# Five late strips a head on VectorE, with the chain's last step in the next head

## The chip, the cores and the metric

The kernel runs on one core of one Trainium2 chip. Its time is the device time of the whole program in microseconds. TensorE is called PE here and in the rows (PEld are its weight loads), VectorE is DVE, ScalarE is ACT, GpSimd is POOL and SyncE, which issues the DMAs, is SP.

## The reference

Two blocks on x of shape (2, 2048, 512), float32: attention with a memory term, then a feed-forward product with weights and activations rounded to float8.

```python
h = layernorm(x)
q, k, v = h @ Wq.T, h @ Wk.T, h @ Wv.T            # 4 query groups x 8 heads x 16; 8 heads x 16
probs = softmax(einsum('bsqhd,bthd->bqhst', q, k) / sqrt(16))
a_dot = einsum('bqhst,bthd->bsqhd', probs, v)
sigma_q = elu(q.reshape(b, s, 4, 128))
a_mem = sigma_q @ memory / (sigma_q @ memory_norm)
x = x + a_dot * (1 - w) + a_mem * w               # w = sigmoid(memory_weight)
x = x + float8_round(layernorm(x) / s) * s @ (weight * weight_scale).T
```

For each batch, head and query group there are 2048 x 2048 scores, and every one needs an exponential. That is most of the work.

## The kernel before

**Heads and strips.** After a preparation (projections, norms, transposes) the kernel runs 64 "heads": 8 chunks of 512 query tokens (NG) times 8 attention heads. One head n computes scores of 4 query groups x 512 tokens against 2048 keys. They are cut into 64 strips; a strip is 128 keys (on the partitions) by the 512 queries of one group, 512 float32 in one bank of PSUM. Strip s has key tile s // 4 and group s % 4. Heads 0 to 62 run in the pipeline described here, the last one in a form of its own that the change leaves alone. There is no row maximum: a guard value in the operands keeps the exponent in range, and the row sum comes out of the weighing, from a column of ones beside the values.

**Units.** Most strips go in units of two or three. PE writes the scores of a unit (pair_scores, third_scores, L1028), ScalarE takes the exponential of the whole unit in one activation (L865, 1536 or 1024 elements a partition), and two or three units later PE weighs it: it multiplies the probabilities with the values into the accumulators (weigh, L1153). The table UNITS_OF_HEAD writes the row out for even and odd heads, WEIGH_BEHIND and WEIGHED_LATER say how many units later each is weighed. Units alternate between two sets of PSUM banks. A unit of two leaves its third bank free; some of these units have an extra in it: "memory" (memory_products: the memory term of half a chunk, units 0 and 2 of even heads), "product" (ffn_product: the feed-forward product of one tile of 128 tokens, unit 2 of odd heads from head 11 on; in head 7 units 2 and 4 turn the weight instead) and "late".

**Late strips.** Four units of two, units 10 to 13 of an even head and 7 to 10 of an odd one, have "late" in their third bank: one strip of the *next* head's last key tile (LATE_TILE, four strips, LATE = 4). ScalarE never sees these. VectorE takes each from PSUM (take_late, L1593) into the buffer late_x and computes the exponential of all four at once by integer and polynomial steps, called the chain: two masks (L1598, L1601), then four two-tensor steps (L1603, L1608, L1610, L1612), each over 2048 elements. The first half is chain_begin, the second chain_end; the result goes to late_probs, a part of the tensor pool. In the next head PE weighs it, one strip behind each of units 14 to 17 (weigh_late, WEIGH_LATE_AT). The step at L1608 waits until PE has weighed the late strips of the head before (late_weighed).

**What releases what.** scores(u) waits for the activation of unit u - 2. The third strip of a unit of three waits (third_free) until the extra that was in its bank has been read. held_in_third finds that extra by going back two units at a time:

```python
def held_in_third(u):
    u -= SLOTS
    while u >= SLOTS and UNITS[u].width < WIDE and UNITS[u].extra is None:
        u -= SLOTS
    return UNITS[u].extra, UNITS[u].number
```

The extras are read by VectorE: late strips by take_late, the memory term by add_memory (L1724, L1728), the feed-forward product by ffn_out (L1716), which raises y_ready. The turned weight is read by copy_ffn_weight.

**VectorE's order.** Each engine runs its instructions in the order in which they are written. VectorE's list for head n is: add_memory(n) in even heads; take_sums(n - 1), which waits until PE has weighed the whole of the head before (pv_done) and moves both accumulators out of PSUM (L1631, raises acc_read, for which PE's first weighing of head n waits); add_memory(n + 1) in even heads; add_sums(n - 1), four small steps; in even heads moments and the rounding to float8 of one tile (round_to_float8, into xq_now) or, in the first chunk, the decoding of the weight; ffn_out or copy_ffn_weight in odd heads that have one; then late_exponentials(n + 1), the four takes and the whole chain. SP turns the rounded tile by DMA (turn_tile), and waits for y_ready too.

## Time and profile before

| | us |
|---|---|
| median of 3 runs | 1939.13 |
| lowest and highest run | 1934.77, 1944.62 |
| the profiled execution | 1942.58 |
| its span, first to last instruction | 1940.5 |

| engine | busy us | share |
|---|---|---|
| PE | 1863.9 | 96% |
| ACT | 1833.6 | 94% |
| DVE | 1409.9 | 73% |
| POOL | 107.2 | 6% |

The heads fill the stretch from 170 us to the end; the preparation is before it. The granted clock of PE is 1.0 of full speed throughout. An engine's busy share is an average, and PE's ends are modelled, so what bounds a stretch is read from who waits for whom. "Idle before" a group of instructions is time of its own engine, with the instruction that ended it.

### The profile page before, as it was taken

To read this page: it belongs to the slowest core of one execution; us is meant where nothing else is said; L and a number is where in the kernel's file an instruction comes from. 1 tells how busy PE (TensorE), PEld (TensorE's weight loads), DVE (VectorE), ACT (ScalarE), POOL (GpSimd) and SP (SyncE) were. 2 spreads that over 40 slices of the span, in tenths; PEclk is the share of its full clock that TensorE was granted. 3 is DMA by queue.
4 is the path that set the end of the run, shared out by engine and by line. 5 is a ranking of instruction groups with operands and counts; after the bars stand their busy time and mean duration, and the time that the engine had idled before them with its cause. 6 is when DMAs were issued, how large, how long until landed. Compare 5 with 4: busy or idle time off the path is not lost.

```text
span 1940.5 us, 115379 instructions
## 1 busy us (share of the span) xinstructions
PE 1863.9 (96%) x54988; PEld 1162.0 (60%) x54996; DVE 1409.9 (73%) x1833; ACT 1833.6 (94%) x1596; POOL 107.2 (6%) x150
## 2 busy tenths in 40 slices
PE   8999999999999999999999999999999999999998
PEld 7885555556565555555555555555655555555555
DVE  6675777777777777787777777777777777777755
ACT  5556999999999999999999999999999999999997
POOL 5541000000000000000000000000000000000000
PEclk9999999999999999999999999999999999999999
DMA  6654111121112211222112211212112211222111
GB/s 220 201 187 153 54 54 40 45 57 45 54 41 56 78 49 42 56 58 64 47 49 56 78 47 44 57 46 76 44 53 57 78 50 41 56 50 72 43 47 46
DMA packets 131327, 130.38 MB, mean 67 GB/s; under 512 B 30451, under 2 KB 106455, under 8 KB 130855
## 3 DMA queue, kind: packets, MB, share of 16 engines
q1 hardware_dynamic: 129847, 121.15, 21.2%
q8 instruction: 431, 7.06, 1.6%
q10 hardware_dynamic: 1008, 1.84, 0.3%
q14 instruction: 41, 0.34, 0.1%
HBM read 86.96 MB, written 32.24 MB: 61 GB/s over the span
## 4 chain that ended last, share of the span: by engine, by line
ACT 76%; PE 21%; issue 2%; DVE 1%; POOL 0%; DMA 0%; ACTq 0%; DVEq 0%; POOLq 0%
ACT pool L865 74%; PE ps L1153 8%; PE ps L945 6%; PE ps L1028 4%; ACT pool L872 1%; PE ps L1200 1%; PE ps L918 1%; DMA resid<-in_x 0%; PE ps L984 0%; POOL q_sq L727 0%; PE ps L909 0%; POOL xn L704 0%; PE ps L926 0%; DVE v_tiles L1608 0%; DVE v_tiles L1610 0%
## 5 line engine op out<-in xcount | busy, mean ns | idle before, releaser
L865 ACT ACTIVATE pool<-ps 128x1536 f32<-128x1536 f32 (+1 forms) x1388 | 1710.1, 1413 | 17.0 <-PE ps L1028 14.7
L1153 PE MATMUL ps<-pool,v_st 64*32 64x128 f32 (+2 forms) x35744 | 1398.3, 357 | 14.7 <-issue 13.7
L1153 PEld LDWEIGHTS ps<-pool,v_st 64*32 64x32 f32 x35744 | 854.5, 106 | 210.0 <-issue 54.3
L1028 PE MATMUL ps<-q_st,k_st 51*32 51x512 f16 x16128 | 903.6, 381 | 49.0 <-ACT pool L865 11.6
L1028 PEld LDWEIGHTS ps<-q_st,k_st 51*32 51x32 f16 x16128 | 246.0, 89 | 474.3 <-ACT pool L865 427.5
L1593 DVE TENSOR_SCALAR late<-ps 128x512 int32<-128x512 f32 x248 | 171.6, 692 | 212.5 <-PE ps L1028 212.5
L1608 DVE SCALAR_TENSOR_TENSOR v_tiles<-late 128x2048 f32<-128x2048 f32 x62 | 142.1, 2293 | 148.1 <-PE ps L1153 144.7
L1612 DVE SCALAR_TENSOR_TENSOR pool<-v_tiles,late 128x2048 f32<-128x2048 f32 x62 | 142.1, 2292 | 2.1
L1610 DVE SCALAR_TENSOR_TENSOR v_tiles<-v_tiles,late 128x2048 f32<-128x2048 f32 x62 | 142.1, 2292 | 2.1
L1603 DVE SCALAR_TENSOR_TENSOR late<-late 128x2048 f32<-128x2048 f32 x62 | 141.6, 2285 | 0.0
L747 POOL TENSOR_TENSOR rstd<-var_eps,minus_half 128x1 f32<-128x1 f32 x32 | 23.0, 720 | 1696.8 <-DVE var_eps L1672 1696.8
L1631 DVE STREAM_TRANSPOSE by_token<-ps 128x512 f32<-128x512 f32 x126 | 82.7, 695 | 32.4 <-PE ps L1153 32.3
L1601 DVE TENSOR_SCALAR late<-late 128x2048 int32<-128x2048 int32 x62 | 76.1, 1228 | 2.1
L1598 DVE TENSOR_SCALAR late<-late 128x2048 int32<-128x2048 int32 x62 | 76.1, 1227 | 2.1
L792 ACT ACTIVATE parts<-ps 128x512 f16<-128x512 f32 x40 | 23.9, 597 | 44.0 <-PE ps L945 44.0
L1492 DVE SCALAR_TENSOR_TENSOR y_out<-epos,ps 128x512 f32<-128x512 f32 x32 | 22.0, 688 | 46.4 <-ACT epos L801 46.3
L945 PE MATMUL ps<-x_high,wqT 128*128 128x512 f32 x128 | 51.6, 403 | 0.0
L945 PE MATMUL ps<-x_high,wq_low 128*128 128x512 f32 x128 | 49.9, 390 | 0.0
L945 PE MATMUL ps<-x_low,wqT 128*128 128x512 f32 x128 | 46.2, 391 | 0.0
L1200 PE MATMUL ps<-mem_aug,wqT 128*32 128x129 f32 x1024 | 41.4, 279 | 0.3
L1728 DVE SCALAR_TENSOR_TENSOR resid<-ps,rnorm,resid 128x128 f32<-128x128 f32 x128 | 39.0, 347 | 2.3
L1200 PEld LDWEIGHTS ps<-mem_aug,wqT 128*32 128x32 f32 x1024 | 24.2, 109 | 25.2 <-DVE resid L1728 17.4
(169 smaller groups left out, 955.1 us busy)
## 6 DMA issues: line engine op xcount, KB each, us to landing
v_st<-v_aug SPq DMA_DIRECT2D x64, 256.0 KB, 3.5
q_st<-q_aug SPq DMA_DIRECT2D x127, 128.0 KB
k_st<-k_aug SPq DMA_DIRECT2D x127, 128.0 KB
sigma_kept<-y_out SPq DMA_DIRECT2D x32, 256.0 KB, 2.0
q_aug<-parts SPq DMA_DIRECT2D x32, 256.0 KB, 2.7
wqT<-sigma_kept SPq DMA_DIRECT2D x32, 256.0 KB, 3.8
q_st<-q_aug SPq DMA_DIRECT2D x127, 64.0 KB
k_st<-k_aug SPq DMA_DIRECT2D x127, 64.0 KB
```

What stands on the lines that cost most here:

```text
L865: act.activation(probs[:, u % HELD, 0:UNITS[u].width * CH], scored(u).rearrange("p a b -> p (a b)"), ACT.Exp, bias=LIFT, scale=EXP_UNIT / ...
L945: return pe.matmul(bank(c, o), w, (x_high, x_low)[x_part][:, par, k, :], start=(k == 0 and p == 0), stop=(k == KT - 1 and p == len(PASSES) ...
L1028: return pe.matmul(ps[VW * c:VW * c + VW, bank, :], k_st[RT * r:RT * r + AUG, n % 2, keys:keys + VW], q_st[RT * r:RT * r + AUG, n % 2, q * ...
L1153: last = pe.matmul(acc[r][VW * c:VW * c + VW, :].rearrange("v (i s) -> v i s", s=VW)[:, places, :], v_st[rows, n % 2, j, :], by_place[rows ...
L1200: last = pe.matmul(am[VW * c:VW * c + VW, t * (KV + 1):(t + 1) * (KV + 1)], sigma_st[:, tokens:tokens + VW], mem_aug[:, :], start=True, st ...
L1593: dve.tensor_scalar(late_x[:, x * CH:x * CH + CH].bitcast(I32), extra_bank("late", number), -2.0 ** 23 / OCTAVE, LOWEST, ALU.mult, ALU.min ...
L1598: dve.tensor_scalar(part.bitcast(I32), fixed.bitcast(I32), MANTISSA, QUARTER, ALU.bitwise_and, ALU.bitwise_or).then_inc(late_step, 1)
L1603: dve.scalar_tensor_tensor(part, part, POWER[0], part, ALU.add, ALU.mult).then_inc(late_step, 1)
L1608: dve.scalar_tensor_tensor(grown, part, POWER[1], part, ALU.add, ALU.mult).then_inc(late_step, 1)
L1610: dve.scalar_tensor_tensor(grown, grown, POWER[2], part, ALU.add, ALU.mult).then_inc(late_step, 1)
L1612: return dve.scalar_tensor_tensor(dst, grown, POWER[3], power, ALU.add, ALU.mult)
L1631: last = dve.transpose(by_token[:, r, :, :, :].rearrange("p q t v -> p (q t v)"), acc[r])
```

## The change

Five strips of each head are now late strips: the last key tile's four and the last strip of the tile before (LATE_STRIPS). The rows of units are now constants EVEN_HEAD and ODD_HEAD, each with one late unit of two more and one unit of three fewer; there are 22 units in a head as before. Head 0, which has no late strips of its own, gets 25 units instead of 24. Late units are 9 to 13 of an even head and 7 to 11 of an odd one. Late strips are weighed behind units 12 to 16. Which units are weighed one unit later is set anew.

The chain is cut differently. late_powers is the first half, late_polynomial two steps of the second, with wait for late_weighed as before; both steps write to late_probs itself instead of late_y, which is gone. The last step is a function of its own, finish_late(n), called in the list of head n, not in that of head n - 1: first in even heads, and between take_sums and add_sums in odd ones. xq_now has moved into the place of k_sq, and pool and late have new sizes.

```diff
-LATE_TILE = ST - 1
-LATE = QG
+HEAD_STRIPS = ST * QG
+LATE_STRIPS = tuple(range(HEAD_STRIPS - QG, HEAD_STRIPS)) + (HEAD_STRIPS - QG - 1,)
+LATE = len(LATE_STRIPS)
...
-UNITS_OF_HEAD = (["2memory", "3", "2memory"] + ["3"] * 7 + ["2late"] * 4 + ["3"] * 8,
-                 ["3", "3", "2product", "3", "2spare", "3", "3"] + ["2late"] * 4 + ["3"] * 11)
+EVEN_HEAD = ["2memory", "3", "2memory"] + ["3"] * 6 + ["2late"] * LATE + ["3"] * 8
+ODD_HEAD = ["3", "3", "2product", "3", "2spare", "3", "3"] + ["2late"] * LATE + ["3"] * 10
 WEIGH_BEHIND = 2
-WEIGHED_LATER = ((0, 1, 2), (0, 1, 2, 3, 9))
-WEIGH_LATE_AT = 14
+WEIGHED_LATER = ((0, 1, 2, 10, 11, 12), (0, 1, 2, 3))
+WEIGH_LATE_AT = 12
...
+def forms_of_head(n):
+    if n == 0:
+        return ["2"] * EARLY_UNITS + EVEN_HEAD[:-1] + ["2", "2"]
+    return (EVEN_HEAD, ODD_HEAD)[n % 2]
...
-            def chain_end(step, width, dst):
-                power, part, grown = late_x[:, 0:width], late_z[:, 0:width], late_y[:, 0:width]
+            def late_polynomial(step):
                 dve.wait_ge(late_step, step + 3)
-                dve.scalar_tensor_tensor(grown, part, POWER[1], part, ALU.add, ALU.mult).then_inc(late_step, 1)
+                dve.scalar_tensor_tensor(late_probs, late_z, POWER[1], late_z, ALU.add, ALU.mult).then_inc(late_step, 1)
                 dve.wait_ge(late_step, step + 4)
-                dve.scalar_tensor_tensor(grown, grown, POWER[2], part, ALU.add, ALU.mult).then_inc(late_step, 1)
-                dve.wait_ge(late_step, step + 5)
-                return dve.scalar_tensor_tensor(dst, grown, POWER[3], power, ALU.add, ALU.mult)
+                dve.scalar_tensor_tensor(late_probs, late_probs, POWER[2], late_z, ALU.add, ALU.mult).then_inc(late_step, 1)
...
-                chain_begin((n - 1) * CHAIN_STEPS, LATE * CH)
-                if n == 1:
-                    for par in range(2):
-                        dve.wait_ge(v_stored[par], 16 * (NG // 2 + 1))
-                else:
+                late_powers((n - 1) * CHAIN_STEPS)
+                if n > 1:
                     dve.wait_ge(late_weighed, n - 1)
-                chain_end((n - 1) * CHAIN_STEPS, LATE * CH, late_probs).then_inc(late_ready, 1)
+                late_polynomial((n - 1) * CHAIN_STEPS)
+
+            def finish_late(n):
+                dve.wait_ge(late_step, n * CHAIN_STEPS)
+                dve.scalar_tensor_tensor(late_probs, late_probs, POWER[3], late_x, ALU.add, ALU.mult).then_inc(late_ready, 1)
...
                 if n % 2 == 0:
+                    if n > 0:
+                        finish_late(n)
                     add_memory(n)
                 if n > 0:
                     take_sums(n - 1)
                 if n % 2 == 0:
                     add_memory(n + 1)
+                else:
+                    finish_late(n)
                 if n > 0:
                     add_sums(n - 1)
```

VectorE where an odd head with a feed-forward product begins, before; by_token is the target of take_sums, head_out of add_sums, y_out that of ffn_out:

```order
L1612 SCALAR_TENSOR_TENSOR pool<-v_tiles,late 128x2048 [waits late_step]
L1631 STREAM_TRANSPOSE by_token<-ps 128x512 [waits pv_done]
L1631 STREAM_TRANSPOSE by_token<-ps 128x512
L1637 TENSOR_TENSOR head_out<-by_token 128x272 [waits acc_read]
L1640 RECIPROCAL rden<-head_out 128x16 [waits halves_added]
L1642 TENSOR_TENSOR head_out<-head_out,rden 128x16x16 [waits rden_ready]
L1647 TENSOR_TENSOR resid<-resid,head_out 128x4x4x16 [waits head_out_ready]
L1716 SCALAR_TENSOR_TENSOR y_out<-ps,scalars,resid 128x512 [waits y_stored,ffn_ready]
```

The same place of VectorE's order now:

```order
L1636 STREAM_TRANSPOSE by_token<-ps 128x512 [waits pv_done]
L1636 STREAM_TRANSPOSE by_token<-ps 128x512
L1631 SCALAR_TENSOR_TENSOR pool<-pool,late 128x2560 [waits late_step]
L1642 TENSOR_TENSOR head_out<-by_token 128x272 [waits acc_read]
L1645 RECIPROCAL rden<-head_out 128x16 [waits halves_added]
L1647 TENSOR_TENSOR head_out<-head_out,rden 128x16x16 [waits rden_ready]
L1652 TENSOR_TENSOR resid<-resid,head_out 128x4x4x16 [waits head_out_ready]
L1721 SCALAR_TENSOR_TENSOR y_out<-ps,scalars,resid 128x512 [waits y_stored,ffn_ready]
```

The chain's last step has moved from ahead of take_sums to behind it, and so stands between take_sums and all that follows.

PE at unit 6 of such a head, before (L1028 writes scores, a pair in 8 products and a third strip in 4; L1153 weighs):

```order
L1028 MATMUL ps<-q_st,k_st 32x512 [waits probs_ready]
L1028 MATMUL ps<-q_st,k_st 32x512 x7
L1028 MATMUL ps<-q_st,k_st 32x512 [waits y_ready]
L1028 MATMUL ps<-q_st,k_st 32x512 x3
L1153 MATMUL ps<-pool,v_st 32x384 [waits probs_ready]
L1153 MATMUL ps<-pool,v_st 32x384 x7
L1153 MATMUL ps<-pool,v_st 32x128 [waits probs_ready]
L1153 MATMUL ps<-pool,v_st 32x128 x15
```

PE at unit 6 now:

```order
L1034 MATMUL ps<-q_st,k_st 32x512 [waits probs_ready]
L1034 MATMUL ps<-q_st,k_st 32x512 x7
L1034 MATMUL ps<-q_st,k_st 32x512 [waits y_ready]
L1034 MATMUL ps<-q_st,k_st 32x512 x3
L1159 MATMUL ps<-pool,v_st 32x384 [waits probs_ready]
L1159 MATMUL ps<-pool,v_st 32x384 x7
L1159 MATMUL ps<-pool,v_st 32x128 [waits probs_ready]
L1159 MATMUL ps<-pool,v_st 32x128 x15
```

Here nothing has moved: the third strip of unit 6 waits for the reading of the feed-forward product, before and now.

VectorE where an even head begins, before, from the end of the late chain to the first part of the memory term (rnorm, resid):

```order
L1608 SCALAR_TENSOR_TENSOR v_tiles<-late 128x2048 [waits late_step,late_weighed]
L1610 SCALAR_TENSOR_TENSOR v_tiles<-v_tiles,late 128x2048 [waits late_step]
L1612 SCALAR_TENSOR_TENSOR pool<-v_tiles,late 128x2048 [waits late_step]
L1724 RECIPROCAL rnorm<-ps 128x2 [waits am_ready]
L1728 SCALAR_TENSOR_TENSOR resid<-ps,rnorm,resid 128x128 [waits rnorm_ready]
```

And now:

```order
L1614 SCALAR_TENSOR_TENSOR pool<-late 128x2560 [waits late_step,late_weighed]
L1616 SCALAR_TENSOR_TENSOR pool<-pool,late 128x2560 [waits late_step]
L1631 SCALAR_TENSOR_TENSOR pool<-pool,late 128x2560 [waits late_step]
L1729 RECIPROCAL rnorm<-ps 128x2 [waits am_ready]
L1733 SCALAR_TENSOR_TENSOR resid<-ps,rnorm,resid 128x128 [waits rnorm_ready]
```

In an even head the last step keeps its place in the row; the steps are wider and write to another tensor.

## Rows read from the trace of the kernel before

**Rows 1.** The page: busy time of each engine over the span.

```profile
PE 1863.9 (96%) x54988; PEld 1162.0 (60%) x54996; DVE 1409.9 (73%) x1833; ACT 1833.6 (94%) x1596; POOL 107.2 (6%) x150
```

**Rows 2.** Waits, 480 to 1870 us: us in total, times, longest.

```profile
PEld ps L1028 <- ACT pool L865: 340.7, 723, 0.8
...
ACT pool L865 <- PE ps L1028: 10.8, 19, 2.0
```

**Rows 3.** Timeline of ScalarE: start us, us, engine, line, what.

```profile
1008.24 1.12 ACT L865 ACTIVATE pool<-ps 128x1024 f32<-128x1024 f32 x1
...
1011.90 1.54 ACT L865 ACTIVATE pool<-ps 128x1536 f32<-128x1536 f32 x1
...
1025.23 1.23 ACT L865 ACTIVATE pool<-ps 128x1024 f32<-128x1024 f32 x1
```

**Rows 4.** Heads 31 and 30 as stretches: us, busy of each engine.

```profile
1022.57:1050.52 27.95, 26.55 (x853) 16.39 (x845) 17.85 (x18) 27.46 (x23) 0.00 (x0) 1.00 0.21 59
995.43:1022.57 27.14, 26.48 (x867) 15.80 (x866) 23.00 (x33) 27.09 (x24) 0.72 (x1) 1.00 0.15 42
```

**Rows 5.** Groups by line and shape: busy us, mean ns | idle before.

```profile
L865 ACT ACTIVATE pool<-ps 128x1536 f32<-128x1536 f32 x1008 | 1387.5, 1525 | 16.7 <-PE ps L1028 14.5
...
L865 ACT ACTIVATE pool<-ps 128x1024 f32<-128x1024 f32 x380 | 385.9, 1118 | 0.3 <-PE ps L1028 0.3
...
L1593 DVE TENSOR_SCALAR late<-ps 128x512 int32<-128x512 f32 x248 | 171.6, 692 | 212.5 <-PE ps L1028 212.5
L1608 DVE SCALAR_TENSOR_TENSOR v_tiles<-late 128x2048 f32<-128x2048 f32 x62 | 142.1, 2293 | 148.1 <-PE ps L1153 144.7
...
L1598 DVE TENSOR_SCALAR late<-late 128x2048 int32<-128x2048 int32 x62 | 76.1, 1227 | 2.1
```

**Rows 6.** Timeline of VectorE around the start of odd head 31.

```profile
1024.31 1.31 DVE L1631 STREAM_TRANSPOSE by_token<-ps 128x512 f32<-128x512 f32 x2 [0.84 <-PE ps L1153]
...
1027.22 0.74 DVE L1716 SCALAR_TENSOR_TENSOR y_out<-ps,scalars,resid 128x512 f32<-128x512 f32 x1
```

**Rows 7.** Timeline of ScalarE: units 0 and 6 of head 31.

```profile
1022.57 1.63 ACT L865 ACTIVATE pool<-ps 128x1536 f32<-128x1536 f32 x1
...
1029.86 1.54 ACT L865 ACTIVATE pool<-ps 128x1536 f32<-128x1536 f32 x1
```

**Rows 8.** Timeline at PE's unit 6 (PEld: weight loads), heads 31, 61.

```profile
1028.76 0.13 PEld L1028 LDWEIGHTS ps<-q_st,k_st 51*32 51x32 f16 x12 [0.34 <-ACT pool L865]
...
1028.99 0.38 PE L1028 MATMUL ps<-q_st,k_st 51*32 51x512 f16 x1
...
1847.72 0.74 DVE L1716 SCALAR_TENSOR_TENSOR y_out<-ps,scalars,resid 128x512 f32<-128x512 f32 x1
...
1849.27 0.13 PEld L1028 LDWEIGHTS ps<-q_st,k_st 51*32 51x32 f16 x12 [0.33 <-ACT pool L865]
```

**Rows 9.** Timeline at the memory bank of even head 32.

```profile
1051.50 0.61 DVE L1728 SCALAR_TENSOR_TENSOR resid<-ps,rnorm,resid 128x128 f32<-128x128 f32 x2
...
1052.38 0.13 PEld L1200 LDWEIGHTS ps<-mem_aug,wqT 128*32 128x32 f32 x4 [0.53 <-DVE resid L1728]
```

**Rows 10.** Timeline: scores of PE and the activation that waited.

```profile
1034.43 0.38 PE L1028 MATMUL ps<-q_st,k_st 51*32 51x512 f16 x2
...
1035.27 1.45 ACT L865 ACTIVATE pool<-ps 128x1536 f32<-128x1536 f32 x1 [0.20 <-PE ps L1028]
```

**Rows 11.** Chain in order of time: start us, us, what.

```profile
1032.05 0.67 PE ps L1153 x15
...
1033.08 0.52 PE ps L1153 x25
```

**Rows 12.** Who waited for the turned weight's tile: us, times.

```profile
  PEld ps L1210: 1.3, 1
```

**Rows 13.** Timeline of VectorE, late chain in head 31.

```profile
1044.44 2.29 DVE L1608 SCALAR_TENSOR_TENSOR v_tiles<-late 128x2048 f32<-128x2048 f32 x1 [4.62 <-PE ps L1153]
...
1049.10 2.29 DVE L1612 SCALAR_TENSOR_TENSOR pool<-v_tiles,late 128x2048 f32<-128x2048 f32 x1
```

More of the change, by code:

```diff
@@ L99, in extra_of @@
     return None, 0
+def forms_of_head(n):
+    if n == 0:
+        return ["2"] * EARLY_UNITS + EVEN_HEAD[:-1] + ["2", "2"]
+    return (EVEN_HEAD, ODD_HEAD)[n % 2]
 def units_of(n):
     units, strip, names = [], 0, []
-    for form in ["2"] * EARLY_UNITS * (n == 0) + UNITS_OF_HEAD[n % 2]:
+    for form in forms_of_head(n):
         width, name = int(form[0]), form[1:]
@@ L238, in attention_ffn @@
         k_sq = sb("k_sq", [P, CH], BF16)
+        xq_now = k_sq
         v_tiles = sb("v_tiles", [P, 2, HEADS, TPC, VW], F32)
@@ L245, in attention_ffn @@
         sigma_st = wqT[:, 0, :].bitcast(F32)
-        late_y = v_tiles[:, :, :, :, :].rearrange("p a h t w -> p (a h t w)")
         wkv_raw = sb("wkv_raw", [P, 2, DM], F32)
@@ L284, in attention_ffn @@
             v_turn = early("v_turn", [P, CH], F32)
-        pool = sb("pool", [P, 8192], F32)
+        pool = sb("pool", [P, (HELD * WIDE + LATE) * CH], F32)
         late = sb("late", [P, 2 * LATE * CH], F32)
@@ L292, in attention_ffn @@
         xqT = sb("xqT", [P, KT, P], BF16)
-        xq_now = sb("xq_now", [P, DM], BF16)
         probs = pool[:, 0:HELD * WIDE * CH].rearrange("p (a b) -> p a b", a=HELD)
@@ L1144, in late_scored @@
                     pe.wait_ge(operands_loaded[n % 2], (n // 2 + 1) * 16 * SCORE_LOADS)
-                third_scores(u, n, LATE_TILE * QG + x).then_inc(late_scores, 1)
+                third_scores(u, n, LATE_STRIPS[x]).then_inc(late_scores, 1)
             def weigh(n, j, held, first_strip, strips, first=False, last_strips=False):
@@ L1177, in weigh_late @@
                 pe.wait_ge(late_ready, n)
-                last = weigh(n, LATE_TILE, late_probs[:, x * CH:x * CH + CH], x, 1)
+                j, q = divmod(LATE_STRIPS[x], QG)
+                last = weigh(n, j, late_probs[:, x * CH:x * CH + CH], q, 1)
                 if x == LATE - 1:
@@ L1594, in take_late, with late_powers @@
                                   -2.0 ** 23 / OCTAVE, LOWEST, ALU.mult, ALU.min).then_inc(late_taken, 1)
-            def chain_begin(step, width):
-                fixed, part = late_x[:, 0:width], late_z[:, 0:width]
+            def late_powers(step):
+                fixed, part = late_x, late_z
                 dve.tensor_scalar(part.bitcast(I32), fixed.bitcast(I32), MANTISSA, QUARTER,
```

## The prediction

> **What bounds the kernel now.** I read the page first: ScalarE is busy 94% of the span, VectorE 73% [rows 1]. PE shows 96%, but its ends are modelled, so the waits decide: the weight loads of PE's scores wait 340.7 us for ScalarE in the 1390 us in the middle, ScalarE waits 10.8 us for those scores [rows 2]. So ScalarE's row of exponentials is the clock. Then its cadence: four activations of 1024 elements from 1008.24 to 1011.90, ten of 1536 to 1025.23 [rows 3]: 0.915 us for a unit of two strips, 1.33 us for one of three. A head (16 wide and 6 narrow units) should last 26.8 us; an even head lasts 27.14 us and the odd one after it 27.95 us [rows 4]. The 0.3 to 1.1 us over is time in which ScalarE waited.
>
> **The strip taken from ScalarE.** In heads 1 to 62 one wide unit becomes a narrow one: 62 x (1.33 - 0.915) = 62 x 0.415 = **-25.7 us**. Head 0 keeps its 64 strips but in 25 units: three more narrow, two fewer wide, 3 x 0.915 - 2 x 1.33 = +0.1 us. The mean durations (1525 against 1118 ns [rows 5]) give 0.407 each, the other bound: -25.2 us. The Trainium skill, page "ScalarE: Activation LUTs", section "What ACT_TABLE_LOAD costs", gives 0.833 ns for each element: an estimate of 427 ns for 512 of them, and of -26.4 us for this term.
>
> **What VectorE takes on.** A head's late work grows from four strips to five. One two-tensor step of the chain goes from 2.293 us [rows 5] to 2.87 us at 5/4 of the width. From two widths (0.74 us for the 512 of ffn_out [rows 6], 2.293 for 2048) it would be 2.81, the other bound. The Trainium skill, page "VectorE: DVE Perf Modes", section "Side-by-side: where the cycles go for N=2048 bf16", counts one element a cycle and about 158 cycles more: an estimate of 2.83 us for 2560. A head's late work (4 takes of 0.69, two masks of 1.23, four steps of 2.29 [rows 5]) is 14.4 us and becomes 18.0. In a pair of heads VectorE is busy 17.85 + 23.00 = 40.9 of 55.1 us [rows 4]; then 48.1 of 54.3. In sum it fits; the order decides.
>
> **The moved step in odd heads, the term that decides.** There VectorE's order was: the chain's last step, take_sums, add_sums, the FFN result (ffn_out), then the new late strips. take_sums waited 0.84 us for PE and started at 1024.31 [rows 6], so the chain's last step ahead of it was covered and cost nothing. Now it stands behind take_sums, ahead of add_sums and ffn_out, which wait for nothing there. take_sums can't start earlier, since PE's last weighing of the head before releases it. So ffn_out ends one step of 2.87 us later. It ended at 1027.22 + 0.74 = 1027.96 [rows 6], 5.39 us after the head's first activation at 1022.57 [rows 7]; now at 8.26.
>
> Who waits for it? In PE's order the third strip of the head's seventh unit (unit 6) waits on y_ready: it writes the bank that held the FFN product (unit 4 has two strips and leaves that bank alone). PE came there at 1028.76 [rows 8], 0.80 us after ffn_out's end. In head 61, the last such, it is 1849.27 against 1847.72 + 0.74 = 1848.46 [rows 8], 0.81. So the 26 odd heads from 11 to 61 have 0.8 us of slack, and 2.87 are taken from it. Behind the waiting instruction stand PE's weighings and its next scores, and ScalarE waits for the strip itself.
>
> When does ScalarE get unit 6? Release: add_memory's last step ended at 1051.50 + 0.61 = 1052.11, PE's load that waited for it started at 1052.38 [rows 9]: 0.26 us. Strip to activation: pair and third strip started at 1034.43 and the activation that waited for them at 1035.27 [rows 10], 0.84 us, of which the pair is 0.22 (1028.76 to 1028.99 [rows 8]); so 0.62. Unit 6 starts 8.26 + 0.26 + 0.62 = 9.14 us into the head, and started at 1029.86 - 1022.57 = 7.29 [rows 7]. That is 1.85 us, x 26 = **+48.1 us**. With the shorter step it is 46.5.
>
> After that PE has no lead. It owes the third strip (0.22), a weighing of three strips (0.67), a split one (0.52) and the next pair (0.22) with 0.4 to hand over, some 2.0 us, against 0.62 + 1.33 = 1.95 of cover. Then two narrow units each ask 0.22 + 0.67 + 0.22 = 1.11 us of PE (weighings from the chain [rows 11]) against 0.915 of ScalarE, 0.2 each. I take 0.4 a head, **+10 us**; the ends are 0 and, if four of the five narrow units fall behind, 0.8 or +21.
>
> **The weight head (7).** The same shift meets the copies of the turned weight. PE waited 1.3 us for those already [rows 12], so nothing covers it: **+2.9 us**, once.
>
> **The even heads.** Here the moved step stands where it stood, ahead of add_memory, only wider. What pays for it is that late weighing now ends at unit 16, not 17. VectorE sat idle 4.62 us for that weighing and went on at 1044.44 [rows 13], 21.9 us into the head. Ahead of it lie now nine wide and seven narrow units, before eleven and six: 1.75 us less, so 20.1. The masks and the first step are done by then: before, 4.62 us earlier, at 17.25; the fifth narrow unit adds 0.9 and the wider masks and step 1.1, so 19.3. Three steps of 2.87 from 20.1 and 0.1 between them end at 28.8. This head lasts 27.95 - 0.42 = 27.5, so they end 1.3 us into the even head, before 1049.10 + 2.29 - 1050.52 = 0.87 [rows 13]. The memory bank comes free 0.45 us later. PE already waited 0.53 us for it [rows 9] without holding ScalarE. I charge 0.2 us a head for this and for the five narrow units in a row: 31 x 0.2 = **+6 us**; ends 0 and 0.45, or +14. In odd heads the late result is ready some 6 us in and wanted at unit 12, past 14 us: nothing.
>
> The chain's middle steps write elsewhere at the same width, xq_now has another place, SyncE's turn of the tile waits for ffn_out and goes 2.9 us later, far ahead of its use two heads on: nothing, and no more than that step's delay if it were on the path.
>
> **The sum.** -25.7 + 0.1 + 48.1 + 10 + 2.9 + 6 = +41 us. The profiled execution took 1942.6 us (its span 1940.5), so 1984; the median of the runs shown is 3.5 us lower, so **1980 us**. Low end: -25.7 + 46.5 + 2.9 = +24, or 1963; if the 0.8 us by which the odd head exceeds the even one [rows 4] falls in part into the new wait, 0.2 x 26 less, 1958. High end: -25.2 + 48.1 + 21 + 3 + 14 = +61, or 2000; with the same 0.2 the other way about 2002 to 2005. I take 2002.
>
> **Rivals.** *The bank's release does not hold ScalarE* (faster). PE would have to reach the third strip so late that the FFN result's delay stays covered; it decides at 0.8 us, any shift under that is free. Then -25.7 + 6 + 0.1 = -20, or 1920 us. For it: ScalarE is the clock and the strip is really gone. Against it: the slack is the same 0.8 in heads 31 and 61, and the step is 2.87. 6%.
> *The delay is half absorbed* (same). take_sums had 0.84 us of idle; if PE delivered the sums earlier by all of that and lost no lead after, the wait is 1.0 us: 26 x 1.0 + 2.9 + 6 - 25.6 = +9, 1948 us, or 1943 with the 0.2 a head. Against it: what PE has to do before that weighing is unchanged. 5%.
> *VectorE becomes the clock* (much slower). If the chain ends 1 us later than worked out, memory banks and sums hold PE by that in 31 heads: +31, or 2011 us. It decides where take and masks end after 20.1 us instead of at 19.3. For it: 48.1 of 54.3 us busy. Against it: in this forecast product heads grow by 1.8 us, which gives VectorE room. 9%.
> That the change does not do what it says is ruled out by the order of instructions: steps of 2560 and five takes in each head.
>
> **How the numbers follow.** The forecast's case has 80% and the range 1958 to 2002; the rivals' centres lie outside it. 0.5%, about what a measurement of this kernel can tell from no change, is 9.7 us: faster 6%, same 5%, slower 89%.
>
> **What would show it.** ffn_out starts 2.9 us later after its head's first activation; PE's load at unit 6 names VectorE's y_out as what it waited for, some 2 us in each of 26 heads; ScalarE has a gap of 1.8 to 1.9 us ahead of unit 6 and small ones after it. Odd heads without a product and even heads last 26.6 to 27.0 us, the odd product heads 29 to 29.5. Were product heads under 27.5 us, the bank's step would be wrong; were the even heads over 27.5, the late chain's.

## The result and the profile after

| | before | after |
|---|---|---|
| median, lowest to highest of 4 runs, us | 1940.85 (1934.77 to 1944.62) | 2004.97 (2004.01 to 2008.66) |
| profiled execution | 1942.58 | 2005.04 |
| its span | 1940.5 | 2003.0 |

The ratio is 1.0337, with a 95% interval from 1.0306 to 1.0368: the kernel became slower by 64 us. I had predicted 1980 us and a range up to 2002. The direction was right, 25 us were missing, and the time lies 3 us above the range. (Before has one run more here than where the prediction was made, so its median is 1940.85 and not 1939.13.)

The page of after, busy time of each engine (answers to [rows 1]):

```profile
PE 1860.3 (93%) x56532; PEld 1240.7 (62%) x56532; DVE 1609.1 (80%) x1895; ACT 1826.8 (91%) x1597; POOL 106.9 (5%) x150
```

ScalarE is busy for 7 us less, and the span is 62 us longer: the time is in its gaps. Waits of after, 480 to 1870 us, the same view as [rows 2] (us in total, times, longest):

```profile
PEld ps L1034 <- ACT pool L871: 238.8, 505, 0.8
...
PEld ps L1159 <- issue: 76.8, 129, 2.6
ACT pool L871 <- PE ps L1034: 64.3, 85, 2.1
...
PEld ps L1034 <- DVE y_out L1721: 42.8, 25, 1.7
PE ps L1159 <- issue: 30.5, 47, 2.3
PEld ps L1034 <- issue: 25.6, 30, 2.6
```

PE's wait for ScalarE, the sign that ScalarE is the clock, fell from 340.7 to 238.8 us; ScalarE's wait for PE rose from 10.8 to 64.3 [rows 2]. Two things are new: the 42.8 us for y_out, which I had named, and the rows with "issue", waits without a releaser. In before they read:

```profile
PEld ps L1153 <- issue: 46.4, 94, 2.6
...
PE ps L1153 <- issue: 13.1, 19, 2.2
...
PEld ps L1028 <- issue: 6.1, 11, 1.4
```

Together 65.6 us before and 132.9 after. (Rows of PE and of PEld can tell of the same stretch, so these sums count some time twice; the count further down does not.) Nothing in my prediction speaks of them.

**The count by heads.** From the starts of all activations in the trace I took the time from each to the next, less 1.3425 us for a unit of three and 0.917 for one of two. (An undisturbed unit takes 1.331 and 0.904, so it counts as -0.01.) What is left is the stall ahead of the next unit. The means of even heads here and below are over heads 12 to 60 and those of product heads over 13 to 59, where nothing else is given; the differences are sums over all heads of a kind. In us:

| mean of a head | before | after | heads | difference of the sums |
|---|---|---|---|---|
| even heads | 0.13 | 1.50 (1.13 in heads 2 to 10) | 31 | +41 |
| odd heads with a product | 0.66 | 2.33 | 26 | +43 |
| head 7 | 1.29 | 6.05 | 1 | +5 |
| odd heads 1, 3, 5, 9 | 0.35 | 0.43 | 4 | 0 |

The stalls of heads 1 to 62 are 23.0 us before and 112.0 after, +89.0. The strip that ScalarE no longer has gives back 62 x (1.3425 - 0.917) = 26.4. That is +62.6, and these heads grew from 1695.9 to 1758.5 us.

Below, a stall "ahead of unit 14" lies between the starts of units 13 and 14. The expectations recorded before each run mostly name a stall by the unit in front of it, one number lower.

### The profile page after: what moved, and what is told of

Its sections match the earlier page's. It is cut to its first block, busy times and chain, and to the rows that moved or that the text cites. A ratio compares the mean times of both kernels' runs of the same rounds, so it can differ in the third digit from the quotient of the medians.

```text
span 2003.0 us, 118521 instructions
## 1 busy us (share of the span) xinstructions
PE 1860.3 (93%) x56532; PEld 1240.7 (62%) x56532; DVE 1609.1 (80%) x1895; ACT 1826.8 (91%) x1597; POOL 106.9 (5%) x150
## 4 chain that ended last, share of the span: by engine, by line
PE 46%; ACT 39%; DVE 11%; issue 4%; POOL 0%; DMA 0%; ACTq 0%; DVEq 0%; POOLq 0%
ACT pool L871 37%; PE ps L1159 24%; PE ps L1034 13%; PE ps L951 6%; DVE pool L1631 4%; DVE by_token L1636 2%; ACT pool L878 1%; PE ps L1207 1%; DVE y_out L1721 1%; DVE pool L1614 1%; DVE pool L1616 1%; DVE head_out L1647 1%; PE ps L924 1%; DVE head_out L1642 0%; DVE rden L1645 0%
## 5 line engine op out<-in xcount | busy, mean ns | idle before, releaser
L1159 PE MATMUL ps<-pool,v_st 64*32 64x128 f32 (+2 forms) x37280 | 1433.1, 349 | 37.4 <-issue 35.1
L1159 PEld LDWEIGHTS ps<-pool,v_st 64*32 64x32 f32 x37280 | 910.5, 106 | 222.9 <-issue 95.6
L1034 PE MATMUL ps<-q_st,k_st 51*32 51x512 f16 x16128 | 955.7, 381 | 86.6 <-DVE y_out L1721 36.7
L1034 PEld LDWEIGHTS ps<-q_st,k_st 51*32 51x32 f16 x16128 | 320.7, 90 | 437.4 <-ACT pool L871 320.4
L1600 DVE TENSOR_SCALAR late<-ps 128x512 int32<-128x512 f32 x310 | 214.4, 692 | 141.3 <-PE ps L1034 133.4
L1614 DVE SCALAR_TENSOR_TENSOR pool<-late 128x2560 f32<-128x2560 f32 x62 | 175.2, 2826 | 47.3 <-PE ps L1159 44.1
L1616 DVE SCALAR_TENSOR_TENSOR pool<-pool,late 128x2560 f32<-128x2560 f32 x62 | 175.2, 2825 | 2.1
L1610 DVE SCALAR_TENSOR_TENSOR late<-late 128x2560 f32<-128x2560 f32 x62 | 174.8, 2819 | 0.0
L1631 DVE SCALAR_TENSOR_TENSOR pool<-pool,late 128x2560 f32<-128x2560 f32 x62 | 173.8, 2804 | 1.1
L1608 DVE TENSOR_SCALAR late<-late 128x2560 int32<-128x2560 int32 x62 | 92.6, 1494 | 2.1
L1605 DVE TENSOR_SCALAR late<-late 128x2560 int32<-128x2560 int32 x62 | 92.6, 1494 | 2.1
L1207 PEld LDWEIGHTS ps<-mem_aug,wqT 128*32 128x32 f32 x1024 | 24.2, 109 | 30.2 <-DVE resid L1733 22.4
```

Source lines behind the costliest of these rows:

```text
L1034: return pe.matmul(ps[VW * c:VW * c + VW, bank, :], k_st[RT * r:RT * r + AUG, n % 2, keys:keys + VW], q_st[RT * r:RT * r + AUG, n % 2, q * ...
L1159: last = pe.matmul(acc[r][VW * c:VW * c + VW, :].rearrange("v (i s) -> v i s", s=VW)[:, places, :], v_st[rows, n % 2, j, :], by_place[rows ...
L1600: dve.tensor_scalar(late_x[:, x * CH:x * CH + CH].bitcast(I32), extra_bank("late", number), -2.0 ** 23 / OCTAVE, LOWEST, ALU.mult, ALU.min ...
L1605: dve.tensor_scalar(part.bitcast(I32), fixed.bitcast(I32), MANTISSA, QUARTER, ALU.bitwise_and, ALU.bitwise_or).then_inc(late_step, 1)
L1608: dve.tensor_scalar(fixed.bitcast(I32), fixed.bitcast(I32), EXPONENT, ONE, ALU.bitwise_and, ALU.bitwise_xor).then_inc(late_step, 1)
L1610: dve.scalar_tensor_tensor(part, part, POWER[0], part, ALU.add, ALU.mult).then_inc(late_step, 1)
```

## The product heads: the wait that was predicted, in a smaller size

Heads 31 and 30 of after, the windows that answer to [rows 4] (from and to, length, then PE, PEld, DVE, ACT, POOL busy):

```profile
1049.68:1079.37 29.69, 26.17 (x856) 18.24 (x860) 22.57 (x19) 27.13 (x24) 0.00 (x0) 1.00 0.20 54
1021.42:1049.68 28.26, 26.59 (x900) 17.11 (x884) 24.43 (x33) 27.01 (x24) 0.72 (x1) 1.00 0.16 44
```

Odd head 31 lasts 29.69 us where the forecast had 29 to 29.5; the even head 28.26 where it had at most 27.0. Timelines of VectorE, PE's loads and ScalarE at the start of head 31, whose first activation is at 1049.67 (start, us, engine, line, what, idle before):

```profile
1049.67 1.49 ACT L871 ACTIVATE pool<-ps 128x1536 f32<-128x1536 f32 x1
...
1051.26 1.31 DVE L1636 STREAM_TRANSPOSE by_token<-ps 128x512 f32<-128x512 f32 x2 [2.55 <-PE ps L1159]
1052.50 2.78 DVE L1631 SCALAR_TENSOR_TENSOR pool<-pool,late 128x2560 f32<-128x2560 f32 x1
1055.20 0.43 DVE L1642 TENSOR_TENSOR head_out<-by_token 128x272 f32<-128x272 f32 x1
...
1056.76 0.74 DVE L1721 SCALAR_TENSOR_TENSOR y_out<-ps,scalars,resid 128x512 f32<-128x512 f32 x1
...
1057.55 0.10 PEld L1034 LDWEIGHTS ps<-q_st,k_st 51*32 51x32 f16 x4 [1.70 <-DVE y_out L1721]
```

```profile
1055.49 1.54 ACT L871 ACTIVATE pool<-ps 128x1536 f32<-128x1536 f32 x1
1058.00 1.45 ACT L871 ACTIVATE pool<-ps 128x1536 f32<-128x1536 f32 x1 [0.98 <-PE ps L1034]
```

The chain's last step stands between take_sums and add_sums, ffn_out ends at 1057.50, PE's load of unit 6 starts 0.05 us later, and ScalarE goes 2.51 us from unit 5 to unit 6 instead of 1.34. The stall ahead of unit 6 is the same in every product head, 1.18 us in the mean. Ahead of units 8 and 9, behind the first narrow ones, stand 0.17 each.

## The even heads: stretches without a releaser

In the even heads the stall sits ahead of unit 14 (0.29 us, in each head) and ahead of units 15 to 18, where it has another size in each head: 0.03, 0.34, 0.46, 0.19 in the mean. Head 30 of after, timeline of PE's loads and ScalarE:

```profile
1039.26 0.43 PEld L1159 LDWEIGHTS ps<-pool,v_st 64*32 64x32 f32 x32 [0.74 <-issue]
...
1040.86 2.79 ACT L871 ACTIVATE pool<-ps 128x1536 f32<-128x1536 f32 x2 [0.46 <-PE ps L1034]
...
1043.00 0.18 PEld L1159 LDWEIGHTS ps<-pool,v_st 64*32 64x32 f32 x15 [1.18 <-issue]
...
1044.34 2.79 ACT L871 ACTIVATE pool<-ps 128x1536 f32<-128x1536 f32 x2 [0.68 <-PE ps L1034]
```

Twice PE stands still between instructions that wait for nothing, and 1.3 to 1.6 us later ScalarE is short of scores. The late strips are weighed here, one strip at a time: each costs 16 loads and 16 products in the trace, as many as three strips of one tile that are weighed together, whose products have 384 columns for 128. PE needs more instructions for the same columns.

**Where the stretches lie.** I counted PE's loads and products from the program's start and looked where loads without a wait start over 0.3 us after the one before, between 480 and 1850 us. Their count, modulo 256, is about 185 at 480 us and drifts evenly to 113 at 1850 us in after, and from 178 to 103 in before, whichever head, unit or line they fall in; a straight line through them misses none by more than 2. The other kernels lie within 10 of these, but for single stretches and for the kind named at e7. So it is not the work at that place; it is every 256th instruction, at some of its occurrences. The queue that brings instructions to the chip has this row in section 3 of the page (packets, MB, share), of before and, below it, of after:

```profile
q8 instruction: 431, 7.06, 1.6%
```

```profile
q8 instruction: 443, 7.26, 1.5%
```

7.06 MB in 431 packets are 16 KB each. PE has 109984 loads and products before and 113064 after: 3080 more, and 12 packets more, which is 257 for each. Nearly every stretch of this kind ends 1.2 to 1.6 us after an instruction packet has landed, and 2.2 to 3.2 us after that packet started; a packet takes 0.9 to 1.6 us. Between a packet's start and the end of a stretch PE started 115 to 169 loads and products (the middle half of after's stretches). I read these together so: PE's instructions come in blocks of 256, the packet for the next block starts with that many of the present one left, and where PE goes through these in less than the 2.2 to 3.2 us, it stands until the block is there. Before has 45 such stretches of 35 us in sum, beside 332 packets in that time; after has 94 of 87 us, beside 328.

**Whether they cost ScalarE anything.** In after's 31 even heads 30.8 us of stall stand ahead of units 15 to 21. Of these, 29.6 us end within 1.7 us behind such a stretch; of the 168 places there without a stall, 14 do. In the odd heads it is 21.0 of 23.2 us. The stall ahead of unit 14 is of another kind: it is in each head, mostly with no such stretch behind it. And PE has no lead to lose there: in before its loads wait 0.50 us a head for ScalarE while that is in units 13 to 17 of an even head, in after 0.00.

## The experiments

Two parts of the change are suspected: the moved step in odd heads, and the finer, earlier weighing of the late strips. "Both edits" below means e1's and e2's together. Times are medians, with the ratio to before on the same chip and its 95% interval.

**e1, the moved step behind ffn_out** (and behind the copies of the turned weight in head 7).

```diff
                 if n % 2 == 0:
                     add_memory(n + 1)
-                else:
-                    finish_late(n)
                 if n > 0:
                     add_sums(n - 1)
...
                         copy_ffn_weight(unit.number)
+                if n % 2 == 1:
+                    finish_late(n)
                 if n + 1 < LAST_HEAD:
```

> The changed kernel, with the chain's last step of odd heads moved behind ffn_out (and behind the copies of the turned weight in head 7); all else as changed, 2005 us. Theory 1 (the product's bank): the 1.18 us gap ahead of unit 6 and the 0.35 us at units 7 and 8 go in 26 heads, -40 us, and about -4 us in head 7: 1961 us; the gaps at units 13 to 17 of even heads stay (1.2 us a head). Rival (the time PE waited there only hid other delays): under half of it comes back, 1985 us or more, with the gaps at units 12 to 18 of odd heads grown.

Measured: 1973.53 us, 1.0160 (1.0133 to 1.0187), 31 us below after. The gap ahead of unit 6 fell from 1.18 to 0.01 us and those ahead of 8 and 9 to 0; head 7 went from 32.61 to 28.25 us. So the mechanism is shown: the moved step holds the bank where the prediction said, at 1.18 us a head in place of 1.85. It gave 12 us less than I expected. The product heads' stall went from 2.33 to 1.13, not to 0.7: the stalls ahead of units 13 to 19 grew from 0.9 to 1.2, and even heads stayed at 1.53. What was no longer lost ahead of unit 6 was lost in part to stretches without a releaser later in the head; there are 115 of 103 us in place of 94 of 87:

```profile
PEld ps L1159 <- issue: 87.8, 143, 3.0
```

**e2, late strips weighed in groups of two, two and one**, behind units 12, 14 and 16, with 36213 products in the program for 37205, and 109096 loads and products in the trace for 113064; the columns are the same.

```diff
+LATE_GROUPS = {0: (0, 2), 2: (2, 2), 4: (4, 1)}
...
             def weigh_late(n, x):
+                if x not in LATE_GROUPS:
+                    return
                 pe.wait_ge(late_ready, n)
-                j, q = divmod(LATE_STRIPS[x], QG)
-                last = weigh(n, j, late_probs[:, x * CH:x * CH + CH], q, 1)
-                if x == LATE - 1:
+                y, strips = LATE_GROUPS[x]
+                j, q = divmod(LATE_STRIPS[y], QG)
+                last = weigh(n, j, late_probs[:, y * CH:(y + strips) * CH], q, strips)
+                if y + strips == LATE:
                     last.then_inc(late_weighed, 1)
```

> The changed kernel, 2005 us, but PE weighs the five late strips in three groups (two strips behind unit 12, two behind unit 14, one behind unit 16) instead of one by one. The same columns go through PE, in 36213 instead of 37205 products of the program (as many weight loads fall away). Theory 2 (PE's instructions arrive in blocks of 256 and it runs dry where they are short and many): the irregular gaps at units 14 to 17 of even heads (0.95 us a head) and 12 to 18 of odd ones (0.8) shrink by half or more: -25 to -40 us, 1965 to 1980. Rival (the gaps are PE's array work crowded into units 12 to 16, or the late chain of VectorE): the columns are the same, so within 5 us of 2005.

Measured: 1969.46 us, 1.0130 (1.0101 to 1.0159), 35.5 us below after. The even heads went from 1.50 to 0.65 us, the gap ahead of unit 14 from 0.29 to 0.06; the gap ahead of unit 6 of product heads is still 1.18. 94 stretches of 87 us became 79 of 63. The two edits work at different places.

**e3, both edits**, run twice.

> Both edits on the changed kernel: last step behind ffn_out, late strips weighed in groups of two. If theory 1 and theory 2 both hold they add: 2005 - 44 - 25 to 40 = 1921 to 1936 us, faster than the kernel before (1941). If the instruction supply is not the cause: 1961 as the first edit alone.

> The run with both edits once more, beside the others on one chip: 1932 us, 0.4 per cent faster than the kernel before.

Measured: 1931.98 us, 0.9958 (0.9940 to 0.9976), and 1929.72 us, 0.9947 (0.9928 to 0.9965). This beats both kernels. It is 73 to 75 us below after, where the two edits alone gave 67 in sum, and 10 to 12 us below before (8 to 10 by the ratios). The stalls of heads 1 to 62 are 35.6 us (32.3 in the second run). Page and waits of e3, 480 to 1870 us:

```profile
PE 1848.2 (96%) x54548; PEld 1150.5 (60%) x54548; DVE 1614.4 (84%) x1895; ACT 1810.6 (94%) x1597; POOL 107.2 (6%) x150
```

```profile
PEld ps L1035 <- ACT pool L872: 312.0, 659, 0.8
...
PEld ps L1160 <- issue: 54.4, 113, 1.9
...
ACT pool L872 <- PE ps L1035: 18.9, 33, 1.4
```

ScalarE waits for PE 18.9 us, near before's 10.8. Of the 26.4 us taken from ScalarE the kernel keeps 8 to 12; the stalls of heads 1 to 62 are 12.6 us above before's.

**e4, before with after's places of late weighing**, to see the earlier weighing alone.

```diff
-WEIGHED_LATER = ((0, 1, 2), (0, 1, 2, 3, 9))
-WEIGH_LATE_AT = 14
+WEIGHED_LATER = ((0, 1, 2, 10, 11, 12), (0, 1, 2, 3))
+WEIGH_LATE_AT = 12
```

> The kernel before (four late strips, 1941 us) with nothing changed but the place of the weighing: late strips behind units 12 to 15 and the changed kernel's list of units that are weighed one later. Theory 2: crowding many short instructions of PE into units 12 to 16 makes gaps in even heads that had none (0.0 us at units 14 to 17): +0.4 to 0.9 us x 31, 1953 to 1968 us. Rival (the even heads' gaps come from the fifth strip: five narrow units in a row or VectorE's wider chain): 1941 us, even heads still without gaps.

Measured: 1954.05 us, 1.0065 (1.0042 to 1.0087). The size was in the expected range, but the place was wrong. Even heads got only 0.17 us ahead of unit 14 and nothing ahead of 15 to 18; it was the product heads that went from 0.66 to 1.12, with 0.64 ahead of unit 15. So the places cost little in even heads by themselves: the irregular stalls there are missing while a head has four late strips and 16 wide units. PE's loads still wait 0.92 us for ScalarE in units 13 to 17 of these heads. The theory "the earlier place costs the even heads" fell here.

**e5, before with its four late strips in two pairs**, e2's edit on before (LATE_GROUPS = {0: (0, 2), 2: (2, 2)}).

> The kernel before (1941 us), with its four late strips weighed two by two (behind units 14 and 16); same columns through PE, 35445 products of the program instead of 36437. Theory 2 (instructions run dry): the irregular gaps at units 14 to 18 of its odd heads, 0.5 us a head, go in good part: -10 to -15 us, 1926 to 1931, which would make the fifth strip worth next to nothing (both edits on the changed kernel took 1932). Rival (the kernel before is not short of instructions, its gaps are DMA or array work): 1939 to 1943 us.

Measured: 1938.49 us, 0.9997 (0.9983 to 1.0011); no change where I had expected 10 to 15 us. The stretches fell from 45 to 24 and the stalls from 23.0 to 18.4 us. The fewer stretches fit the theory; the stalls show nothing, since e6 below has 16.9 us with all its instructions. Before loses little of ScalarE's time to such stretches: 14 us in 62 heads stand behind one. A stretch on PE costs only where PE has no lead.

**e6, before with 128 more instructions ahead of everything**: half a block, with 64 more of the preparation's warm-up transposes.

```diff
-WARM_UP_TURNS = 16
+WARM_UP_TURNS = 80
```

> The kernel before with 64 more warm-up transposes of PE ahead of everything, that is 128 more instructions, half a block of 256; nothing else changes. Counting PE's weight loads and products from the start, PE's idle stretches with no releaser lie in the kernel before at count modulo 256 = 184 at 480 us, drifting to 112 at 1850 us (instructions that the count does not see). Theory 2: the block's edge decides, so they keep these residues though every place in the program has moved by 128, and so fall in other heads and units. Rival (a place in the program or its DMAs makes them): they stay at their heads and units, and the residues become 56 drifting to 240. The time: the start up to 10 us later, else the same within 10 us.

Measured: 1938.26 us, 0.9994 (0.9982 to 1.0006). The counts at which the stretches fall did not move (178 at 480 us and 103 at 1850, as in before; the 184 and 112 of the expectation are after's), though the work stands at other counts now. The stretches moved to other heads: by how much an odd head lasts longer than 26.98 us, before and shifted, head 17 went from 2.41 to 0.43, 25 from 1.81 to 0.04, 37 from 1.60 to 0.03, while 15 went from 0.04 to 0.79 and 45 from 0.04 to 0.84. It is the instruction's number that stalls, not the instruction. In before seven product heads pay 1.0 to 2.4 us, eight 0.2 to 0.8 and eleven next to nothing. Head 31 is one of the seven, and so was 0.8 us longer than its even neighbour [rows 4].

**e7, both edits, but four late strips weighed at once** behind unit 13 and the fifth behind 16 ({1: (0, 4), 4: (4, 1)}), 35717 products in the program: fewer instructions still, in one lump.

> Both edits of the run before (last step behind ffn_out, late strips in groups), but the four late strips of the last key tile are weighed in one group behind unit 13 and the fifth behind unit 16: 35717 products instead of 36213. Theory 2 alone: fewer instructions, 0.2 us a head less in gaps, 1920 to 1930 us. Against it: 0.85 us of array work in one piece behind unit 13 costs a gap of up to 0.5 us there in each head, 1935 to 1955 us. I expect the two about to cancel: 1932, at most 1 per cent either way.

Measured: 1940.58 us, 1.0002 (0.9991 to 1.0012), 9 to 11 us above e3. The irregular stalls ahead of units 15 to 19 of even heads are gone, and a fixed one of 0.91 us stands ahead of unit 14 instead. Timeline of e7 there:

```profile
1004.02 6.10 ACT L872 ACTIVATE pool<-ps 128x1536 f32<-128x1536 f32 x6
1010.81 1.46 ACT L872 ACTIVATE pool<-ps 128x1536 f32<-128x1536 f32 x1 [0.69 <-PE ps L1035]
```

Fewer instructions are no use where they stand in one heap. The reading I take is that PE's turn of that unit is then longer than an activation; e8 below points the same way. Of e7's 58 stretches without a wait 24 are 0.33 us each, at one place of the even heads and at any count: these are not a block's.

**e8, both edits, with WEIGHED_LATER = ((0, 1, 2), (0, 1, 2, 3))**: are the shifted units 10 to 12 of even heads worth it?

> Both edits (last step behind ffn_out, late strips in groups of two), and in even heads units 10, 11 and 12 are weighed two units later as the rest, not three, so that unit 15 no longer has two weighings and a late one. Theory 2: PE's instructions in units 13 to 16 stand less close, gaps there shrink from 0.4 to 0.2 us an even head, -6 us, 1926. Rival (units 12 and 13 are narrow and PE has no room there for a weighing as well): a steady gap of 0.2 to 0.4 us at unit 12 or 13, +3 to +6 us, 1936.

Measured: 1935.55 us, 0.9968 (0.9955 to 0.9982), 6 us above e3's second run, which was on the same chip. Even heads lose 0.88 us for 0.56: 0.37 and 0.17 ahead of units 13 and 14, in each head, while the stalls after them became fewer. In this row of units, weighing 10 to 12 later is right.

**e9, both edits with e6's 128 instructions**: is e3's gain luck of the block boundaries?

> Both edits with 64 more warm-up transposes ahead (128 instructions of PE, half a block). Theory 2: the block edges fall at other places, the sum of the gaps may differ by a few us either way; 1925 to 1940 us. If the gain of the two edits were an accident of where the edges fall, this run is as slow as the kernel before or slower (1940 to 1950).

Measured: 1934.21 us, 0.9958 (0.9945 to 0.9971), beside 0.9947 (0.9928 to 0.9965) for e3. The intervals overlap, and heads 1 to 62 take 1679.8 us where e3's two runs have 1682.1 and 1678.8: with the blocks moved by half the gain is still there, so it is no accident of where they end.

**e10, before with more instructions for the same products.** Each weighing of three strips of one tile is cut in two and one: 40461 products in the program for 36437.

```diff
-                    a, b = max(strip, j * QG), min(end, j * QG + QG)
-                    last = weigh(n, j, probs[:, u % HELD, (a - strip) * CH:(b - strip) * CH], a - j * QG, b - a,
-                                 first=a == 0, last_strips=last_unit and b == end)
+                    lo, hi = max(strip, j * QG), min(end, j * QG + QG)
+                    for a, b in ((lo, hi),) if hi - lo < WIDE else ((lo, hi - 1), (hi - 1, hi)):
+                        last = weigh(n, j, probs[:, u % HELD, (a - strip) * CH:(b - strip) * CH], a - j * QG, b - a,
+                                     first=a == 0, last_strips=last_unit and b == end)
```

> The kernel before (1941 us), with each weighing of three strips in one piece cut into two and one: the same columns through PE in 40461 instead of 36437 products of the program, 11 per cent more, and as many weight loads more. Theory 2: PE uses up a block of 256 instructions faster wherever such units stand in a row, so gaps with no releaser appear in the second half of even heads too, which had none, and those of odd heads grow: +0.5 to 1.5 us a head, 1970 to 2030 us. Rival (PE has room for such instructions and the array's columns are what counts): under +10 us, and no stretches without a releaser in even heads.

Measured: 2056.38 us, 1.0611 (1.0578 to 1.0643), beyond the expected range. Page and waits (480 to 1870 us) of e10:

```profile
PE 1895.1 (92%) x63036; PEld 1358.1 (66%) x63044; DVE 1410.9 (69%) x1833; ACT 1857.5 (91%) x1596; POOL 107.2 (5%) x150
```

```profile
q8 instruction: 494, 8.09, 1.7%
```

```profile
PEld ps L1153 <- issue: 144.6, 241, 3.4
...
ACT pool L865 <- PE ps L1028: 79.7, 142, 3.6
```

PE's busy time grew by 31 us, the span by 109, and the 16096 more loads and products brought 63 more packets, 255 for each. 239 stretches of 193 us stand where before has 45 of 35, and the stalls of heads 1 to 62 grew from 23.0 to 133.4 us, in all sorts of heads. VectorE and ScalarE have the same instructions as before. This shows that the number of PE's instructions alone, at the same columns, costs this kernel time. In heads 12 to 61, 95 of 118 us of stall end within 1.7 us behind such a stretch; of the places without a stall 16% do. The rest may be PE's added busy time, which was not separated. (The stalls ahead of units 8 to 11 of product heads, 0.1 to 0.4 us in the mean, run from 0 to 1.4.)

## Why the prediction was right or wrong

- **ScalarE's strip, -25.7 us: right.** It is 26.4, as worked out above. The Trainium skill, page "ScalarE: Activation LUTs", section "What ACT_TABLE_LOAD costs", gave 427 ns for the 512 elements and the estimate of -26.4; the traces, with 1.331 - 0.904 = 0.427 us, agree.
- **The chain's steps, 2.87 us: right to 0.05.** The groups of after by line:

```profile
L1614 DVE SCALAR_TENSOR_TENSOR pool<-late 128x2560 f32<-128x2560 f32 x62 | 175.2, 2826 | 47.3 <-PE ps L1159 44.1
```

  The scaling by 5/4 was too high by a fixed part, and the estimate of 2.83 us from the Trainium skill, page "VectorE: DVE Perf Modes", section "Side-by-side: where the cycles go for N=2048 bf16", agrees with the trace.
- **The bank's release, +48.1 us: right mechanism, mis-sized.** It measured 1.18 x 26 = 30.7. Unit 6 starts 8.33 us into head 31 and not 9.14. Of these 0.8 us, 0.16 is take_sums, released 1.58 us into the head and not 1.74; 0.17 is the step in its place (2.70 us from its start to the next one's, for 2.87 more); 0.1 is the steps after; 0.21 the release, 0.05 us and not the 0.26 of another bank [rows 9]; 0.17 the way from strip to activation, 0.45 us for 0.62. The other way goes a stall of 0.11 us ahead of unit 3, which before has and after has not. Every term was taken from its nearest row and each row lay on the slow side: that they all did is bad luck, not a step of the reasoning. e1 showed the place.
- **The lost lead, +10 us: right.** The gaps ahead of units 7, 8 and 9 are 0.02, 0.17 and 0.17, 0.36 x 26 = 9.4.
- **Head 7, +2.9 us: low.** Its stall grew by 4.8: 3.7 at the unit that waits for the copy, 0.4 of lost lead behind it, and the rest ahead of units 12 to 17. e1 took the 3.7 away, which shows the cause; why it is 3.7 and not one step's 2.8 was not followed.
- **The end of the late chain: right, in part by luck.** I said 1.3 us into the even head; it is 1.2, from this VectorE timeline of after, ahead of a head that starts at 1079.37:

```profile
1072.05 2.83 DVE L1614 SCALAR_TENSOR_TENSOR pool<-late 128x2560 f32<-128x2560 f32 x1 [2.29 <-PE ps L1159]
...
1077.77 2.83 DVE L1631 SCALAR_TENSOR_TENSOR pool<-pool,late 128x2560 f32<-128x2560 f32 x1
```

  I had the chain end 28.8 us into an odd head of 27.5 us; it ends 30.9 us into one of 29.7. The 27.5 left out the wait at the bank that I had just worked out, and as the chain waits for PE's weighing, both moved by the same 2 us.

  The rival that VectorE becomes the clock fell with it. Its time, 2011 us, was nearer than mine, by a mechanism that is not there: the memory bank holds PE for 22.4 us in 31 heads, and ScalarE for 0.04 us in each.
- **The even heads, +6 us with a high end of 14: the step that failed.** They cost +41: 8 ahead of unit 14 and 32 behind it. My 0.2 us a head was for VectorE's chain and the five narrow units. PE's part of the edit, some 50 loads and products more in a head (3080 / 62) and closer together, stands nowhere in the sum; I put it at nothing without a reason. That PE waited 340.7 us for ScalarE [rows 2] would be none: it is a sum over all places, and while ScalarE is in units 13 to 17 of even heads the wait fell from 0.50 us to 0.00. And I had not looked at PE's instruction count, or at the waits without a releaser, which were 65.6 us in before. e2, which takes 64 loads and products out of each head (3968 / 62) and leaves all else, takes 0.85 of 1.50 us a head away; e10 shows the same loss in before, without any of the change. Of the 0.65 us that remain in e2, 0.24 stand ahead of unit 1, as in before; nearly all the rest is in the same units and of the same irregular kind. My sign "even heads over 27.5 us" did come, 28.0 in the mean, but it named the late chain, which was not at fault.
- **Product heads behind unit 12: not in the sum.** +0.4 us a head of the same irregular kind, less 0.3 that went, most of it ahead of units 3 and 11: with the two terms above it makes the +43, so +3.

The working came out 21 us short: -17 for the bank, +35 for the even heads, +2 for head 7, +3 for the product heads, and small ones. That it was so near is luck: the bank's term was too high by half of what the even heads' was too low. The other 3.5 us of the 25 are what I took off because before's profiled execution lay above its median; after's lies at its median.

**Open.** That blocks of 256 instructions are fetched late is inferred: from the count, from the packets' times, and from e6 and e10. The stall ahead of unit 14 of even heads is left unexplained: e4 gives 0.17 of its 0.29 us to the earlier place, and e2 takes nearly all of it away. No run has five late strips at before's places, so what the fifth strip's instructions cost even heads and what the lost wide unit does is not told apart. No run changes the fetch itself, so nothing here says how many blocks are kept ahead. The count drifts by some 72 between 480 and 1850 us; instructions of PE's that I don't count (waits, branches) may be in the blocks too, which I did not check. Head 0 lasts 29.3 to 31.7 us with before's row of units and 30.0 to 33.4 with after's; that was not followed. Why even heads pay more than odd ones in e3 is not settled either.

## What to carry to other kernels

Slack is local: before an edit is charged at nothing because an engine waits for hundreds of microseconds in sum, look whether it waits in the units where the edit puts work. Where a wait has no releaser in the profile, count instructions, and prefer the form of a product that does the same columns in fewer instructions, but not in one heap: two strips at a time beat both one and four. A step put ahead of an engine's reading of a bank is free only up to the slack of whoever waits for the bank, 0.8 us here for a step of 2.8; e1's order (read the bank first, then the long step) cost one moved line.

## What the runs showed of the hardware

PE's instructions arrive in packets of 16 KB (443 of them for 113064 loads and products in after, 494 for 126080 in e10, 255 for each), and by my reading a block can be late: 94 stretches of 0.3 to 2.7 us in after, nearly all ending 1.2 to 1.6 us after a packet's landing. With 15% more loads and products for the same columns the kernel was 116 us longer (e10), with PE's busy time up by only 31. VectorE's release of a bank reached PE's load in 0.05 us at y_out, and in 0.27 us at the memory bank [rows 9]. ScalarE's cadence in an undisturbed row was 1.331 us for 1536 elements and 0.904 for 1024 in before, after, e3 and e7, while the duration of one activation of 1536 in the trace varied from 1.44 to 1.65 us.
